# Separate semaphores for the loads of x and of the context, and x loaded one batch further ahead

## The chip, the cores and the metric

The kernel runs on one core of one Trainium2 chip. The metric is device time in microseconds (us), the median of three runs. The core has five engines that run their own instruction streams and meet only at semaphores: TensorE (PE in the profile, with its weight loads as PEld), VectorE (DVE), ScalarE (ACT), GpSimd (POOL) and SyncE (SP), which here does nothing but issue transfers (DMAs). An engine's queue, in which its waits and transfer issues stand, is written with a q, as SPq.

## The reference, cut to what matters

```
x = x + attention(layernorm(x), context, context, bias)   # 64 batches, 128 rows x 128; 16 heads of 64
x = x + moe_ffn(layernorm(x))                             # 8 experts of 128 -> 512 -> 128, 32 rows each
```

The 64 batches come as four groups of 16 to the expert layer's expert choice (the x of a batch is 128 rows by 128 columns, its context 120 rows by 128). In the attention, of each batch: q is made of the normalized x; k and v of the context; scores = q kT x 128^-0.5 + bias; softmax over the 120 columns; times v; and a projection back to 128 columns, added to x. The expert layer routes rows by a softmax over 8 logits and the top 32 rows per expert and batch. Everything is held to float32 accuracy, which the kernel reaches with pairs of float16 parts (hi and lo) and three products for one.

## The kernel before, in words

The program has two parts. The attention (function `attention`, lines 74 to 677) goes over the 64 batches; then come routing and the experts, which the change does not touch. The whole of x stays on the chip in `x_sb` (128 rows x 64 batches x 128), so the load of one batch's x has no buffer to wait for. The context of a batch goes to `ctx_f`, which has two buffers, taken in turn.

The attention is a software pipeline written out by hand. Each engine runs slots t = -1 to 68, and a slot has four steps g = 0 to 3, one for each group of four heads. Slots 5 to 62 or so are a loop whose body is two slots. What an engine does in a step is in fixed order, and belongs to several batches at once. In slot t:

- DVE begins step 0 with `bn_stats` of the x of batch t+1 (line 453). Before it stands a wait on `loaded_xc` (line 449). Then in every step: bias and row minimum of the scores (`neg`, line 461, four of them), the reciprocal of the softmax's sum (L498), the low part of v (L503), the attention's output (L518), and at the end of the step the low part of the probabilities of the step before (L545), which sets `p_lo_ready`.
- POOL raises the variance to the power -1/2 (`rstd`, L311), then waits on the same `loaded_xc` (line 314) and splits the context of batch t+1 into hi and lo (L318, L325). It also writes the high part of the probabilities (L288) and the low part of the output (L296).
- ACT does the exponentials (L432) and copies results out of PSUM.
- PE does in each step the scores (L593), v (L578 to L580 into `bk_b`), the projection of an older batch (L620), probabilities times v (L636), and q and k (L578 to L580 into `bk_a`). The projection and probabilities times v need transposed operands, `w_f`.
- SP issues, in slot t and step g, one transposing transfer `w_f<-parts` (L248): it turns the probabilities of batch t-1 and the outputs of an older batch. It waits for four semaphores, of which `p_lo_ready` is that of DVE's line 545. PE uses the result four steps later. Between the transposing transfers SP issues the ordinary loads: after the first (g = 0) the x and then the context of batch t+2 (`load_x`, lines 208 to 217), after the second (g = 1) a piece of the expert weights (`load_ffn`, L227).

Both loads of a batch count on one semaphore, `loaded_xc`, 32 for a batch, so DVE and POOL each wait for both of them. `load_x` itself waits at its head until both loads of all earlier batches have landed, and before the context until the buffer is free (`ctx_ready`). The function `alone` puts an empty instruction after a wait. Below, T0 to T3 are the four transposing transfers of a slot.

Of the kernel before, what the change touches and what calls it, by code (L numbers as in the profile page):

```python
# [73 lines left out]
def attention(nc, v):  # L74
    x, ctx_t, bias, wqkv_t, wp_t, gate_t, ffn_w = (v[n] for n in (
        "x", "ctx_t", "bias", "wqkv_t", "wp_t", "gate_t", "ffn_w"))
# [3 lines left out]
    x_sb, xg_hi, xg_lo, ffn_hi, ffn_lo, logits, ident, ident_h, iota, gate_sb = (v[n] for n in (  # L80
        "x_sb", "xg_hi", "xg_lo", "ffn_hi", "ffn_lo", "logits", "ident", "ident_h", "iota", "gate_sb"))

    with ExitStack() as ctx:
# [3 lines left out]
        def two(name, shape, dt):  # L87
            return [sb(f"{name}{i}", shape, dt) for i in range(2)]
# [4 lines left out]
        sem = v["sem"]  # L93
# [8 lines left out]
        ctx_f = two("ctx_f", [D, K], F32)  # L102
# [35 lines left out]
        xn_turned, x2_turned, gate_out = bk_m[:, 0:128].bitcast(F16), bk_m[:, 128:256], bk_m[:, 256:256 + E]  # L138

        loaded_wv, loaded_wq, loaded_wk = sem("loaded_wv"), sem("loaded_wq"), sem("loaded_wk")  # L140
        loaded_b, loaded_xc, loaded_ffn = sem("loaded_b"), sem("loaded_xc"), sem("loaded_ffn")

        weight_parts = ((loaded_wv, slice(2 * HD, 3 * HD)), (loaded_wq, slice(0, HD)), (loaded_wk, slice(HD, 2 * HD)))
        const_ready = sem("const_ready")
# [28 lines left out]
        def live(b):  # L173

            return not isinstance(b, int) or 0 <= b < B

        def upto(count):

            return min(count, B) if isinstance(count, int) else count

        def some(count):

            return not isinstance(count, int) or count > 0

        def alone(eng):

            eng.nop(nofuse=True)

        def slots(eng, slot, end=last, loop_end=loop_end, first=first):

            for t in range(first, FRONT):
                slot(t, t % 2)
            with eng.Fori(FRONT, loop_end - 1, 2) as t:
                slot(t, FRONT % 2)
                slot(t + 1, (FRONT + 1) % 2)
            for t in range(loop_end, end):
                slot(t, t % 2)

        def behind(t, g, k):

            return t - 1 + (g - k) // GROUPS, (g - k) % GROUPS
# [3 lines left out]
        @block.sync  # L205
        def _(sp):

            def load_x(b, par):

                if some(b):  # L210
                    sp.wait_ge(loaded_xc, 32 * b)
                    alone(sp)
                sp.dma_start(x_sb[:, b, :], x[:, b, :]).then_inc(loaded_xc, 16)
                if some(b - 1):
                    sp.wait_ge(ctx_ready, b - 1)
                    alone(sp)
                sp.dma_start(ctx_f[par][:, :], ctx_t[:, b, :]).then_inc(loaded_xc, 16)

            def load_ffn(b, par):

                if some(b):
                    sp.wait_ge(loaded_ffn, 16 * b)
                if some(b - 1):
                    sp.wait_ge(ffnw_ready, b - 1)
                alone(sp)
                src = ffn_w[:, bass.ds(b * WCH, WCH)] if not isinstance(b, int) else ffn_w[:, b * WCH:(b + 1) * WCH]
                sp.dma_start(wst[par][:, :], src).then_inc(loaded_ffn, 16)  # L227

            def turn(t, g):

                n = 4 * (t - 1) + g
                b5, g5 = behind(t, g, PV_LAG)
                blocks = slice(0 if live(t - 1) else 2 * GH, BLOCKS)
                if not live(t - 1) and not live(b5):
                    return
                if live(t - 1):
                    sp.wait_ge(p_lo_ready, n + 1)
                    alone(sp)
                    if some(n - GROUPS + 1):
                        sp.wait_ge(pv_written, n - GROUPS + 1)  # L240
                    alone(sp)
                if live(b5):
                    sp.wait_ge(o_lo_ready, 4 * b5 + g5 + 1)
                    alone(sp)
                    if some(4 * b5 + g5 - GROUPS + 1):
                        sp.wait_ge(proj_written, 4 * b5 + g5 - GROUPS + 1)
                    alone(sp)
                sp.dma_start_transpose(turned[g][:, blocks, :], parts[g][:, blocks, :].rearrange("p a b -> p (a b)")  # L248
                                       ).then_inc(moved[g], 16)

            def slot(t, par):
                for g in range(GROUPS):
                    turn(t, g)
                    if g == 0 and live(t + 2):
                        load_x(t + 2, par)
                    if g == 1 and live(t + 1):
                        load_ffn(t + 1, (par + 1) % 2)

            load_x(0, 0)
            slots(sp, slot, end=B + 3, loop_end=loop_end - 2)  # L260

        @block.gpsimd
        def _(pool):
# [26 lines left out]
            def lower_o(t, g):  # L290

                b5, g5 = behind(t, g, SPLIT_LAG)
                if live(b5):
                    n = 4 * b5 + g5
                    pool.wait_ge(o_hi_ready, n + 1)
                    pool.tensor_tensor(o_parts[g5][:, 1, :, :], o_sb[g5 % 2][:, :, :], o_parts[g5][:, 0, :, :],  # L296
                                       ALU.subtract).then_inc(o_lo_ready, 1)

            def slot(t, par):
                c = chain(t)  # L300
                i = (par + 1) % 2
                lower_o(t, 0)

                pool.wait_ge(vpe_ready, t + 2)
                alone(pool)
                if some(upto(t + 1)):
                    pool.wait_ge(xn_ready, upto(t + 1))
                if some(t - 4):
                    pool.wait_ge(xn2_ready, t - 4)
                alone(pool)  # L310
                pool.tensor_tensor(rstd[:, :], vpe[:, :], half[:, :], ALU.pow).then_inc(rstd_ready, 1)  # L311
                if live(t + 1):

                    pool.wait_ge(loaded_xc, (t + 2) * 32)
                    if some(4 * t):
                        pool.wait_ge(v_written, 4 * t)
                    alone(pool)
                    pool.tensor_copy(ctx_hi[i][:, :], ctx_f[i][:, :]).then_inc(pool_chain, 1)  # L318
                upper_parts(t, 0)
                lower_o(t, 1)  # L320
                if live(t + 1):

                    pool.wait_ge(pool_chain, c[0])
                    alone(pool)
                    pool.tensor_tensor(ctx_lo[i][:, :], ctx_f[i][:, :], ctx_hi[i][:, :],  # L325
                                       ALU.subtract).then_inc(ctx_ready, 1)

                    pool.wait_ge(xn_ready, t + 2)
                    if some(t + 1):
                        pool.wait_ge(xT_written, t + 1)  # L330
                    alone(pool)
                    pool.tensor_copy(xn_hi[:, :], xn[:, :]).then_inc(pool_chain, 1)
                    pool.wait_ge(pool_chain, c[1])
                    alone(pool)
                    pool.tensor_tensor(xn_lo[:, :], xn[:, :], xn_hi[:, :], ALU.subtract).then_inc(xn_parts_ready, 1)
                upper_parts(t, 1)
                lower_o(t, 2)
                upper_parts(t, 2)
                lower_o(t, 3)
                if live(t - 4):  # L340

                    pool.wait_ge(xg_hi_ready, t - 3)
                    alone(pool)
                    pool.tensor_tensor(xg_lo[:, t - 4, :], xn2[:, :], xg_hi[:, t - 4, :],
                                       ALU.subtract).then_inc(xg_ready, 1)
                upper_parts(t, 3)

            def chain(t):

                hi = 2 * (t + 1) if not isinstance(t, int) else 2 * min(t + 1, B)
                return [1 + hi + (k if live(t + 1) else 0) for k in (1, 2)]

            slots(pool, slot)

        @block.scalar
# [82 lines left out]
        def _(dve):  # L440
            dve.wait_ge(const_ready, 11)

            def step(t, par, g):
# [2 lines left out]
                tw, gw, pw = (t, g - 1, par) if g else (t - 1, GROUPS - 1, (par + 1) % 2)  # L446
                if g == 0 and live(t + 1):

                    dve.wait_ge(loaded_xc, (t + 2) * 32)
                    if some(t + 1):  # L450
                        dve.wait_ge(stats_ready, t + 1)
                    alone(dve)
                    nc.vector.bn_stats(stats[:, 0, :], x_sb[:, t + 1, :]).then_inc(x_stats_ready, 1)
# [98 lines left out]
            def slot(t, par):  # L552
                for g in range(GROUPS):
                    step(t, par, g)
# [734 lines left out]
```

## Time and profile before

| what | value |
|---|---|
| median of three runs | 1084.17 us (1082.05 to 1084.37) |
| the profiled execution | 1082.19 us |
| its span, first to last instruction | 1080.4 us |
| mean granted clock of TensorE | 0.975 of full speed |
| attention, steady stretch looked at | 100 to 640 us from the span's start, 49 slots |
| busy there, of 540 us | PE 527.1, DVE 523.2, ACT 483.5, POOL 385.3 |

A row of instructions gives the line, the engine, the operation, what it writes and reads, how often, the busy time and the mean duration, and then the idle time of the engine just before these instructions and what ended it. Records of one engine overlap where the next instruction begins before the last has drained, so sums of durations run above the busy time. A row of waits gives the waiting engine and line, what it waited for, the total, the number of times and the longest.

### The profile page before, as it was taken

What the parts mean: (1) busy time and instruction counts of PE and PEld (TensorE: products, weight loads), DVE (VectorE), ACT (ScalarE), POOL (GpSimd) and SP (SyncE); (2) the same over time, 40 slices, a digit from 0 to 9 for tenths busy, and PEclk for the clock granted to TensorE, in tenths of its full rate; (3) what the DMA queues carried; (4) which work ended last, traced back from release to release, by engine and by line L of the source; (5) the groups of instructions that cost most, each with busy time, mean ns of one, the idle gap of its engine ahead of it and who ended that gap; (6) DMA issues with size and microseconds to landing.
All of it is one profiled execution on the core that took longest, in us unless ns stands there. A gap on an engine that the chain in (4) does not pass through costs nothing. (4 is left out here: it accounts for less than half of the span.)

```text
span 1080.4 us, 47391 instructions
## 1 busy us (share of the span) xinstructions
PE 1001.7 (93%) x13640; PEld 810.5 (75%) x13640; DVE 895.2 (83%) x3981; ACT 839.0 (78%) x2536; POOL 724.7 (67%) x1086
## 2 busy tenths in 40 slices
PE   4999999999999999999999999983799999999995
PEld 3777888888888888888888888872466666666664
DVE  4999999999999999999999999995756565665553
ACT  5888898888988898888889899881576666666562
POOL 6677677777767676776767676772077667677673
PEclk9999999999999999999999999995599999999998
DMA  3998887888888887888888888892001121111112
GB/s 102 167 149 158 164 169 153 163 166 163 162 163 163 164 168 153 167 164 165 160 162 166 165 165 156 172 162 45 1 21 29 31 69 29 47 48 32 50 49 69
DMA packets 440585, 130.91 MB, mean 121 GB/s; under 512 B 417504, under 2 KB 433888, under 8 KB 440544
## 3 DMA queue, kind: packets, MB, share of 16 engines
q1 hardware_dynamic: 439680, 128.24, 61.0%
q10 hardware_dynamic: 864, 2.16, 0.5%
q8 instruction: 21, 0.34, 0.1%
q14 instruction: 20, 0.16, 0.0%
HBM read 16.58 MB, written 4.19 MB: 19 GB/s over the span
## 5 line engine op out<-in xcount | busy, mean ns | idle before, releaser
L432 ACT ACTIVATE probs<-neg,negmax 128x120 f32<-128x120 f32 x1024 | 320.4, 387 | 76.6 <-DVE negmax L461 76.1
L461 DVE CUSTOM_DVE_ANT_0 neg<-bk_s,bias_sb 128x120 f32<-128x120 f32 x1024 | 226.2, 275 | 3.3 <-PE bk_s L593 2.2
L1136 POOL TENSOR_TENSOR hid<-hid_f,hid 128x512 f16<-128x512 f32 x128 | 167.7, 1314 | 74.4 <-ACT hid L1090 73.4
L288 POOL CAST parts<-probs 128x480 f16<-128x480 f32 x256 | 151.9, 593 | 95.2 <-ACT probs L432 95.2
L296 POOL TENSOR_TENSOR parts<-o_sb,parts 128x256 f16<-128x256 f32 x256 | 172.0, 672 | 48.8 <-ACT parts L397 48.8
L593 PE MATMUL bk_s<-qk 64*128 64x120 f32 x2048 | 181.4, 294 | 8.7 <-DVE negmax L461 4.2
L545 DVE TENSOR_TENSOR parts<-probs,parts 128x480 f16<-128x480 f32 x256 | 171.3, 669 | 0.0
L593 PEld LDWEIGHTS bk_s<-qk 64*128 64x128 f32 x2048 | 136.7, 186 | 32.6 <-issue 13.6
L1190 DVE TENSOR_TENSOR hid_f<-bk_u,silu 128x512 f32<-128x512 f32 x128 | 88.4, 691 | 85.7 <-ACT silu L1083 35.0
L389 ACT COPY qk<-bk_a 128x496 f32<-128x496 f32 x256 | 146.5, 572 | 2.3 <-PE bk_a L580 2.3
L311 POOL TENSOR_TENSOR rstd<-vpe,half 128x2 f32<-128x2 f32 x69 | 77.2, 1118 | 68.2 <-DVE vpe L512 68.2
L636 PE MATMUL bk_o<-v_hi,w_f 120*128 120x65 f16 x1024 | 121.1, 196 | 1.1 <-DMA w_f<-parts 1.1
L638 PE MATMUL bk_o<-v_hi,w_f 120*128 120x65 f16 x1024 | 120.5, 193 | 0.0
L637 PE MATMUL bk_o<-v_lo,w_f 120*128 120x64 f16 x1024 | 120.0, 192 | 0.0
L578 PE MATMUL bk_a<-xT,w_hi 128*128 128x128 f16 x512 | 113.9, 222 | 5.0 <-ACT qk L389 2.2
L620 PE MATMUL bk_y<-wp_hi,w_f 128*128 128x128 f16 x512 | 100.7, 222 | 15.9 <-DMA w_f<-parts 14.7
L1083 ACT ACTIVATE silu<-bk_g 128x512 f32<-128x512 f32 x128 | 78.2, 611 | 44.3 <-PE bk_g L973 42.9
L580 PE MATMUL bk_a<-xT,w_hi 128*128 128x128 f16 x512 | 112.4, 220 | 0.0
L579 PE MATMUL bk_a<-xT,w_lo 128*128 128x128 f16 x512 | 112.3, 219 | 0.0
L1090 ACT CAST hid<-hid_f 128x512 f16<-128x512 f32 x128 | 80.7, 630 | 39.5 <-DVE hid_f L1190 39.2
L397 ACT CAST parts<-o_sb 128x256 f16<-128x256 f32 x256 | 105.9, 414 | 6.7 <-DVE o_sb L518 6.7
L579 PE MATMUL bk_a<-ctx_hi,w_lo 128*128 128x120 f16 x512 | 111.0, 217 | 0.0
(165 smaller groups left out, 3562.9 us busy)
## 6 DMA issues: line engine op xcount, KB each, us to landing
y_all<-y SPq DMA_DIRECT2D x128, 64.0 KB, 2.0
wst<-ffn_w SPq DMA_DIRECT2D x64, 96.0 KB, 2.6
w_f<-parts SPq DMA_TRANSPOSE x260, 3.7
x_sb<-x SPq DMA_DIRECT2D x64, 64.0 KB, 2.3
out<-x_sb SPq DMA_DIRECT2D x16, 256.0 KB, 2.0
ctx_f<-ctx_t SPq DMA_DIRECT2D x64, 60.0 KB, 2.0
w_f<-wqkv_t ACTq DMA_DIRECT2D x3, 512.0 KB, 5.4
wp_sb<-wp_t ACTq DMA_DIRECT2D x1, 512.0 KB, 5.9
```

What stands on the lines that cost most here:

```text
L288: pool.tensor_copy(p_parts[g][:, 0, :, 0:K], probs[g % 2][:, :, :]).then_inc(p_hi_ready, 1)
L296: pool.tensor_tensor(o_parts[g5][:, 1, :, :], o_sb[g5 % 2][:, :, :], o_parts[g5][:, 0, :, :], ALU.subtract).then_inc(o_lo_ready, 1)
L389: nc.scalar.copy(qk[pw][:, gw, :], bk_a[:, 0:QK]).then_inc(qk_ready, 1)
L432: e = nc.scalar.activation(probs[g % 2][:, i, :], neg[g % 2][:, i, :], ACT.Exp, bias=negmax[g % 2][:, i:i + 1], scale=-1.0)
L461: r = nc.vector.tensor_tensor_reduce(out=neg[g % 2][:, i, :], in0=bk_s[i % 2][:, (i // 2) * K:(i // 2 + 1) * K], in1=bias_sb[:, :], scale= ...
L545: nc.vector.tensor_tensor(p_parts[g1][:, 1, :, 0:K], probs[g1 % 2][:, :, :], p_parts[g1][:, 0, :, 0:K], ALU.subtract).then_inc(p_lo_ready, 1)
L579: nc.tensor.matmul(out, ll, rh, start=False, stop=False)
L593: m = nc.tensor.matmul(bk_s[h][:, j * K:(j + 1) * K], qk[p1][r, g, j * S:(j + 1) * S], qk[p1][r, g, GP * S + j * K:GP * S + (j + 1) * K], ...
L636: nc.tensor.matmul(bk_o[:, i * OW:(i + 1) * OW], ph, v_hi[p2][0:K, h, :], start=True, stop=False)
L637: nc.tensor.matmul(bk_o[:, i * OW:i * OW + DH], ph, v_lo[p2][0:K, h, :], start=False, stop=False)
L638: m = nc.tensor.matmul(bk_o[:, i * OW:(i + 1) * OW], pl, v_hi[p2][0:K, h, :], start=False, stop=True)
L1136: nc.gpsimd.tensor_tensor(hid[1][par][:, ic, :], hid_f[ic % 2][:, :], hid[0][par][:, ic, :], ALU.subtract).then_inc(hid_lo_ready, 1)
```

## The change

The semaphore `loaded_xc` becomes two, `loaded_x` and `loaded_ctx`, 16 a batch each. DVE waits on `loaded_x` alone, POOL on `loaded_ctx` alone. The function `load_x` is cut in two. `load_ctx` stays behind the first transposing transfer (g = 0) and loads the context of batch t+2 as before. `load_x` goes behind the fourth (g = 3) and loads the x of batch t+3, so that an x is issued three steps later in the slot but for one batch further on: it comes one step earlier than before with respect to the batch it serves. Each of the two waits until the earlier loads of its own kind have landed. Before the slots, SP issues x of batch 0, context of batch 0, and x of batch 1.

```diff
-            def load_x(b, par):
+            def load_x(b):
                 if some(b):
-                    sp.wait_ge(loaded_xc, 32 * b)
+                    sp.wait_ge(loaded_x, 16 * b)
                     alone(sp)
-                sp.dma_start(x_sb[:, b, :], x[:, b, :]).then_inc(loaded_xc, 16)
+                sp.dma_start(x_sb[:, b, :], x[:, b, :]).then_inc(loaded_x, 16)
+
+            def load_ctx(b, par):
+                if some(b):
+                    sp.wait_ge(loaded_ctx, 16 * b)
+                    alone(sp)
                 if some(b - 1):
                     sp.wait_ge(ctx_ready, b - 1)
                     alone(sp)
-                sp.dma_start(ctx_f[par][:, :], ctx_t[:, b, :]).then_inc(loaded_xc, 16)
+                sp.dma_start(ctx_f[par][:, :], ctx_t[:, b, :]).then_inc(loaded_ctx, 16)
...
                     if g == 0 and live(t + 2):
-                        load_x(t + 2, par)
+                        load_ctx(t + 2, par)
                     if g == 1 and live(t + 1):
                         load_ffn(t + 1, (par + 1) % 2)
-
-            load_x(0, 0)
+                    if g == 3 and live(t + 3):
+                        load_x(t + 3)
+
+            load_x(0)
+            load_ctx(0, 0)
+            load_x(1)
...
-                    pool.wait_ge(loaded_xc, (t + 2) * 32)
+                    pool.wait_ge(loaded_ctx, (t + 2) * 16)
...
-                    dve.wait_ge(loaded_xc, (t + 2) * 32)
+                    dve.wait_ge(loaded_x, (t + 2) * 16)
```

SP's program in the second slot of the loop's body, before: the last two transposing transfers of one slot (T2's end and T3 stand ahead of it), then T0 of the slot shown is the last `DMA_TRANSPOSE` before the loads, and T1 the one behind them.

```order
L237 ISA
L240 REGISTER_ALU [waits p_lo_ready]
L248 DMA_TRANSPOSE w_f<-parts 128x12x128 [waits pv_written,o_lo_ready,proj_written]
L211 ISA
L213 ISA [waits loaded_xc]
L213 DMA x_sb<-x 128x128
L217 ISA [waits ctx_ready]
L217 DMA ctx_f<-ctx_t 128x120
L237 REGISTER_ALU
L240 REGISTER_ALU [waits p_lo_ready]
L248 DMA_TRANSPOSE w_f<-parts 128x12x128 [waits pv_written,o_lo_ready,proj_written]
```

The same place now, from the load of x behind T3 of the slot before, over T0, to T1 (lines are 1 to 11 higher in the changed kernel).

```order
L212 ISA
L214 ISA [waits loaded_x]
L214 DMA x_sb<-x 128x128
L244 ISA
L247 REGISTER_ALU [waits p_lo_ready]
L255 DMA_TRANSPOSE w_f<-parts 128x12x128 [waits pv_written,o_lo_ready,proj_written]
L224 ISA [waits loaded_ctx,ctx_ready]
L224 DMA ctx_f<-ctx_t 128x120
L244 REGISTER_ALU
L247 REGISTER_ALU [waits p_lo_ready]
L255 DMA_TRANSPOSE w_f<-parts 128x12x128 [waits pv_written,o_lo_ready,proj_written]
```

The load of x has left the place between T0 and T1 and stands ahead of T0; the context is now directly behind T0, with one wait more.

SP's program from its start to the first transposing transfer, before.

```order
L213 DMA x_sb<-x 128x128
L217 DMA ctx_f<-ctx_t 128x120
L213 DMA x_sb<-x 128x128 [waits loaded_xc]
L217 DMA ctx_f<-ctx_t 128x120
L227 DMA wst<-ffn_w 128x192
L213 DMA x_sb<-x 128x128 [waits loaded_xc]
L217 DMA ctx_f<-ctx_t 128x120 [waits ctx_ready]
L227 DMA wst<-ffn_w 128x192 [waits loaded_ffn]
L248 DMA_TRANSPOSE w_f<-parts 128x12x128 [waits p_lo_ready]
```

And now.

```order
L214 DMA x_sb<-x 128x128
L224 DMA ctx_f<-ctx_t 128x120
L214 DMA x_sb<-x 128x128 [waits loaded_x]
L224 DMA ctx_f<-ctx_t 128x120 [waits loaded_ctx]
L234 DMA wst<-ffn_w 128x192
L214 DMA x_sb<-x 128x128 [waits loaded_x]
L224 DMA ctx_f<-ctx_t 128x120 [waits loaded_ctx,ctx_ready]
L234 DMA wst<-ffn_w 128x192 [waits loaded_ffn]
L214 DMA x_sb<-x 128x128 [waits loaded_x]
L255 DMA_TRANSPOSE w_f<-parts 128x12x128 [waits p_lo_ready]
```

Four loads of x instead of three stand ahead of the first transposing transfer, and each load waits for the earlier ones of its kind alone.

## Rows read from the trace of the kernel before

**Rows 1.** Stage 100 to 640: engines' busy time as headed, granted clock, DMA share, GB/s.

```profile
core 0: us, PE busy (x) PEld busy (x) DVE busy (x) ACT busy (x) POOL busy (x), PEclk, DMA share, GB/s
100.00:640.00 540.00, 527.12 (x8270) 463.90 (x8267) 523.18 (x2791) 483.49 (x1615) 385.25 (x685) 1.00 0.85 163
```

**Rows 2.** Groups of DVE's instructions, 100 to 640 us: the first of a slot.

```profile
L453 DVE BATCH_NORM_STATS2 stats<-x_sb 128x6 f32 x49 | 14.4, 295 | 16.2 <-DMA ctx_f<-ctx_t 15.2 <-issue 0.7
```

**Rows 3.** Who waited for whom, 100 to 640 us: total us, times, longest.

```profile
ACT probs L432 <- DVE negmax L461: 56.5, 98, 1.0
POOL rstd L311 <- DVE vpe L512: 43.0, 49, 1.3
...
PEld bk_y L620 <- DMA w_f<-parts: 16.5, 48, 0.7
DVE stats L453 <- DMA ctx_f<-ctx_t: 15.2, 40, 0.6
PEld bk_s L593 <- issue: 8.7, 36, 0.4
PEld bk_a L578 <- ACT qk L389: 6.1, 34, 0.2
```

**Rows 4.** Who waited for the loads of `ctx_f`, whole span: us, times.

```profile
  DVE stats L453: 19.4, 47
```

**Rows 5.** DVE in order of time, end of one slot and start of the next.

```profile
304.73 0.74 DVE L545 TENSOR_TENSOR parts<-probs,parts 128x480 f16<-128x480 f32 x1
...
309.71 0.64 DVE L545 TENSOR_TENSOR parts<-probs,parts 128x480 f16<-128x480 f32 x1
310.60 0.29 DVE L453 BATCH_NORM_STATS2 stats<-x_sb 128x6 f32 x1 [0.25 <-DMA ctx_f<-ctx_t]
310.92 0.28 DVE L461 CUSTOM_DVE_ANT_0 neg<-bk_s,bias_sb 128x120 f32<-128x120 f32 x1
```

**Rows 6.** SP's queue in order of time: T0 to T3 and the next T0.

```profile
305.77 1.43 SPq L248 DMA_TRANSPOSE w_f<-parts  x1
307.54 0.58 SPq L213 DMA_DIRECT2D x_sb<-x  x1
308.36 0.33 SPq L217 DMA_DIRECT2D ctx_f<-ctx_t  x1
309.09 1.41 SPq L248 DMA_TRANSPOSE w_f<-parts  x1
310.82 0.63 SPq L227 DMA_DIRECT2D wst<-ffn_w  x1
311.84 1.44 SPq L248 DMA_TRANSPOSE w_f<-parts  x1
...
313.68 1.48 SPq L248 DMA_TRANSPOSE w_f<-parts  x1
...
316.97 1.42 SPq L248 DMA_TRANSPOSE w_f<-parts  x1
```

**Rows 7.** SP's own waits, 100 to 640 us.

```profile
SPq L187 <- DVE parts L545: 47.6, 61, 1.2
```

**Rows 8.** Transfers: KB of one, median us from issue to landing.

```profile
w_f<-parts SPq DMA_TRANSPOSE x260, 3.7
x_sb<-x SPq DMA_DIRECT2D x64, 64.0 KB, 2.3
...
ctx_f<-ctx_t SPq DMA_DIRECT2D x64, 60.0 KB, 2.0
```

**Rows 9.** PE in order of time: scores of step 3 and of the next step 0.

```profile
306.81 0.71 PE L593 MATMUL bk_s<-qk 64*128 64x120 f32 x8
...
309.68 0.71 PE L593 MATMUL bk_s<-qk 64*128 64x120 f32 x8 [0.15 <-issue]
...
310.69 0.22 PE L620 MATMUL bk_y<-wp_hi,w_f 128*128 128x128 f16 x1
```

**Rows 10.** DVE and POOL in order of time: first scores of step 3; split of the context.

```profile
307.77 0.27 DVE L461 CUSTOM_DVE_ANT_0 neg<-bk_s,bias_sb 128x120 f32<-128x120 f32 x1
...
302.91 0.28 POOL L318 CAST ctx_hi<-ctx_f 128x120 f16<-128x120 f32 x1
```

More of the change, by code:

```diff
@@ L140, in attention @@
         loaded_wv, loaded_wq, loaded_wk = sem("loaded_wv"), sem("loaded_wq"), sem("loaded_wk")
-        loaded_b, loaded_xc, loaded_ffn = sem("loaded_b"), sem("loaded_xc"), sem("loaded_ffn")
+        loaded_b, loaded_ffn = sem("loaded_b"), sem("loaded_ffn")
+        loaded_x, loaded_ctx = sem("loaded_x"), sem("loaded_ctx")
         weight_parts = ((loaded_wv, slice(2 * HD, 3 * HD)), (loaded_wq, slice(0, HD)), (loaded_wk, slice(HD, 2 * HD)))
```

## The prediction

> **What bounds the kernel now.** I first read the stages. From 100 to 640 us, PE is busy 527.1 us of 540 and DVE 523.2, at full clock [rows 1]; a slot takes 540 / 49 = 11.02 us (49 is the count of the first instruction of a slot) [rows 2]. Two engines at 97% leave the question which one waits for which, and a busy PE hides stalls, since the ends of its matmuls are modelled. So I next read who waited for whom. In this stretch DVE has one wait, ever: `bn_stats`, the first instruction of a slot, for the load of the context, 15.2 us in 40 of 49 slots [rows 3]. Its idle time there is 16.2 us [rows 2], and the stage leaves 540 - 523.2 = 16.8: DVE's stream is full but for this stall. The others have room: ACT waits 56.5 us for DVE, POOL 43.0 for DVE, PE 16.5 + 8.7 + 6.1 = 31.3 at its weight loads [rows 3]. DVE is the bound, with 0.33 us of stall in a slot.
>
> The reader should see in order of time what the stall is. DVE's step ends at 310.35, and `bn_stats` starts at 310.60 after 0.25 idle, released by the context [rows 5]. The x that it reads was issued at 307.54, the context at 308.36 [rows 6]; at medians of 2.3 and 2.0 us to landing [rows 8], x is there at 309.84 and the context at 310.36, when DVE is ready. DVE waits for a load that it does not read, since both count on one semaphore.
>
> **Part 1: DVE's wait for the context goes.** `bn_stats` now waits for x alone, and on the scale of rows 6 the x issued behind T3, at about 315.5, is for the `bn_stats` one slot after that at 310.60, so at about 321.3 (310.60 + 11.02 - 0.33): 5.8 us ahead, against 2.3 us to landing. The x is never late. In the steady stretch this frees 15.2 us; the 0.7 and the rest of the 16.2 that no transfer ends I leave standing. Outside it, 19.4 - 15.2 = 4.2 us [rows 4] lie in the filling and draining of the pipeline, where other waits are near; bounds 0 and 4.2, I take half, 2.1. Term: -17.3, at most 16.2 + 4.2 = 20.4.
>
> **What is late next on DVE's side.** Scores: PE's scores of step 0 end at 309.68 + 0.71 = 310.39, DVE takes them at 310.92, 0.53 later [rows 5, 9]. Less 0.33 this is 0.20. At step 3 they end at 307.52 and are taken at 307.77 [rows 9, 10], 0.25 later, and there DVE does not wait. So it just fits in this slot. Over a slot PE needs 11.02 less its own waits of 31.3 / 49 = 0.64, that is 10.38; DVE needs 11.02 - 0.33 = 10.69. PE can follow, by 0.31. If all its waits for transposed operands stayed (16.5 / 49 = 0.34), it would need 10.72 and the gain would be 0.30 in a slot for 0.33.
>
> **Part 2: the context moves up behind T0; POOL waits for it alone.** POOL splits it at 302.91, some 2.3 us into a slot [rows 10], and DVE waited for the same load before the slot began, so it has been there for over 2 us. It is issued about 0.8 us earlier now (308.36 against 307.54). Cost nothing; were the cover gone, POOL's 43.0 / 49 = 0.88 us of waiting a slot would come first.
>
> **Part 3: SP's queue.** SP is nearly full: it waits 47.6 us of 540 [rows 7], 0.97 a slot, so its issues take 10.05 of 11.02. Added: one more wait, bounded by 0 and by the whole gap between the end of x's issue and the context's, 308.36 - 308.12 = 0.24; I take 0.12, for the gap holds a wait of the same kind and other instructions. The context's issue, now right behind a transposing one, may take what x takes there (0.58) and not 0.33: 0 to 0.25, I take 0.25, since the weights' load behind T1 takes 0.63 too. That makes 10.42, at most 10.54: under DVE's 10.69. x's own issue fills a gap: from T3's end at 313.68 + 1.48 = 315.16 to the next T0 at 316.97 lie 1.81 us, where a transposing issue that waits for nothing needs about 0.40 (T2's end to T3) [rows 6]. x takes 0.34 + 0.58 = 0.92 with the gap ahead of it, the shorter slot takes 0.33: 0.16 us is left. T0 is held by DVE (its operand ends at 305.47 [rows 5], T0 starts at 305.77), so it does not get later. T1 and T2 come earlier behind T0 by the 0.82 from x's issue to the context's, less 0.25 and 0.12: 0.45. PE needs them 0.33 earlier. So they are no later for PE than now, and its 16.5 us of waits shrink rather than grow. Cost 0 by this, and 0.15 a slot if x's issue is as slow as its neighbours allow (rival one).
>
> Here the page "DMA: Bandwidth & Descriptors" of the Trainium skill (section Issuing engines are not separate DMA queues) says that the issue time on the sequencer is usually small beside the transfer. By that rule SP would never bind and rival one would have no chance. The trace disagrees: a transposing issue holds SP 1.43 us of 3.7 to landing [rows 6, 8], and four with three loads fill 91% of its time. I go by the trace.
>
> **Part 4: the start.** Four loads of x instead of three stand ahead of the first transposing transfer, each waiting for the one before: at most one more landing, 2.3 us, on a queue that waits for DVE then. I take 0, bounds -1 and +1.
>
> **Sum.** Against the profiled execution, 1082.19 us (span 1080.4, 1.8 around it): -17.3 and 0 give 1064.9. The median of the runs stands 2.0 above that execution, one run of three beside it; I add 1 and predict 1066.
>
> **Rivals.**
>
> One: SP or the transposed operands bind next, and about half is kept. For it: only 0.16 us is left ahead of T0, only 0.20 ahead of the scores of step 0. If x's issue and T0's waits come out 0.3 longer, T0 is 0.3 - 0.16, about 0.15, late in every slot and the slot becomes 10.69 + 0.15, so 0.18 a slot is gained: 49 x 0.18 = 9, with nothing at the ends: 1082.2 - 9 + 1 = 1074 (1070 to 1079). Against it: SP's work is 10.42 by the sum.
>
> Two: nothing changes, the stall passes to the scores (L593) or to another wait of DVE that the profile shows at zero because `bn_stats` took it first. For it: PE is 98% busy. Against it: PE waits 0.64 a slot, much of it for DVE itself. 1082 to 1085. That the change does not do what it says belongs here: x would have to be what ended the stall, and at 309.84 it was not.
>
> Three, slower: x now stands right ahead of T0, and T0's data wait for x's. T0 lands at 305.77 + 3.7 = 309.47, and PE needs it at 310.69 [rows 9]: 1.22 of room, 0.89 in the shorter slot. Beyond that delay PE starts late in every slot; from 0.89 + 0.33 = 1.22 on it costs more than is gained. If T0 waited for the whole landing of x, 2.3 less the 0.56 that x's issue ends before it, it would be 1.74 late: +0.52 a slot, 49 x 0.52 = 25, 1108. Against it: T1 stands right behind both loads today, and the median transposing transfer still lands in 3.7.
>
> The same page of the Trainium skill (section Queues, rings and completion order) says that a DMA engine takes descriptors of a queue in ring order. That speaks against the change; by it T0 waits while x's 64 KB move, at the stage's 163 GB/s [rows 1] an estimate of 0.4 us, which is under 0.89. It puts rival three's chance low.
>
> **How the numbers follow.** Forecast 0.65, rival one 0.23, two 0.07, three 0.05. The forecast alone would give 1061 to 1069: the whole 20.4 below, 13 above. The range that holds 8 in 10 takes in rival one's centre: 1060 to 1076. A measurement of this kernel tells 0.2% (2.2 us) from no change. Faster 0.88 (forecast and rival one), same 0.07, slower 0.05.
>
> **What would show it.** In the changed profile DVE's `bn_stats` has no wait for a transfer, and DVE's idle time from 100 to 640 us falls under 3 us; the slot is 10.7 us. The load of x stands between T3 and T0, T1 about 0.45 us earlier behind T0. PE's waits for `w_f` fall under 16.5 us. I am wrong if DVE's idle time comes back at `neg` (L461 before) behind PE, or if SP's waits for DVE fall to nearly nothing while PE waits longer for `w_f`.

## The result

The changed kernel takes 1057.4 us (median of 4 runs, 1056.93 to 1060.19); the kernel before 1084.16 (4 runs). The ratio is 0.9763, 95% interval 0.9742 to 0.9784, so 2.4% faster. A second time, beside the experiments, it took 1056.72 us (5 runs; the kernel before 1084.51 there), ratio 0.9753 (0.9739 to 0.9767). The forecast was 1066 with a range of 1060 to 1076: the direction was right, the time lies below the range. The profiled execution of the changed kernel is the slowest of its four, 1060.19 us with a span of 1058.4; that of the second time took 1055.92 with 1054.1.

From 100 to 640 us the stages show more work in the same time (50.8 slots for 48.9), columns as in [rows 1]:

```profile
100.00:640.00 540.00, 532.02 (x8590) 478.31 (x8588) 539.05 (x2900) 503.06 (x1678) 404.79 (x712) 1.00 0.88 169
```

DVE is busy 539.05 of 540 us, for 523.18 in [rows 1]. Its first instruction of a slot has lost its idle time, 16.2 us in [rows 2] (line 453 is now 464):

```profile
L464 DVE BATCH_NORM_STATS2 stats<-x_sb 128x6 f32 x51 | 14.4, 283 | 0.0
```

The waits of the same stretch, for [rows 3], and then SP's own, for [rows 7]:

```profile
POOL parts L299 <- ACT probs L443: 72.2, 102, 0.8
ACT probs L443 <- DVE negmax L472: 36.5, 101, 0.5
...
POOL rstd L322 <- DVE vpe L523: 23.1, 51, 0.7
PEld bk_y L631 <- DMA w_f<-parts: 15.3, 33, 0.8
PE bk_y L631 <- DMA w_f<-parts: 7.5, 25, 0.5
DVE rsum L509 <- PE bk_o L649: 0.4, 2, 0.2
```

```profile
SPq L188 <- DVE parts L556: 0.5, 3, 0.2
```

The row of DVE waiting for the context is gone; nothing of its size has taken its place on DVE. ACT and POOL wait less for DVE, which comes round sooner. SP waited 47.6 us for DVE before and waits 0.5 now: its queue is nearly without a pause.

In order of time, end of a slot on DVE, for [rows 5]:

```profile
290.45 0.63 DVE L556 TENSOR_TENSOR parts<-probs,parts 128x480 f16<-128x480 f32 x1
291.00 0.28 DVE L464 BATCH_NORM_STATS2 stats<-x_sb 128x6 f32 x1
291.21 0.26 DVE L472 CUSTOM_DVE_ANT_0 neg<-bk_s,bias_sb 128x120 f32<-128x120 f32 x1
```

The last operation of the slot (line 556, 545 before) starts at 290.45 and lasts to 291.08, and `bn_stats` starts at 291.00, before that end. In [rows 5] the same two starts lie 0.89 apart, here 0.55.

SP's queue, for [rows 6]: T0, context, T1, weights, T2 and T3 in one row, x, the next T0.

```profile
287.04 1.45 SPq L255 DMA_TRANSPOSE w_f<-parts  x1
288.95 0.46 SPq L224 DMA_DIRECT2D ctx_f<-ctx_t  x1
289.93 1.43 SPq L255 DMA_TRANSPOSE w_f<-parts  x1
291.69 0.61 SPq L234 DMA_DIRECT2D wst<-ffn_w  x1
292.80 3.31 SPq L255 DMA_TRANSPOSE w_f<-parts  x2
296.46 0.55 SPq L214 DMA_DIRECT2D x_sb<-x  x1
297.43 1.43 SPq L255 DMA_TRANSPOSE w_f<-parts  x1
```

T1 follows T0 after 2.89 us, 3.32 in [rows 6]. On average over the stage it is 2.82 us, 3.42 before. From one T0 to the next it is 10.39 us here and 11.20 there, but these two are unlike: the 11.20 holds the end of the loop's body, the 10.39 does not, and the next T0, behind the loop's end, comes after 10.76.

**Where the time went, slot by slot.** I measured from start to start on DVE, over the 49 slots of the stretch before and 50 after. A slot fell from 11.040 to 10.625 us, by 0.415. From the start of its last operation to the start of `bn_stats` it was 0.965 us and is 0.558: 0.407, nearly all of it. From `bn_stats` to the first `neg` 0.273 became 0.211, and the rest of the slot grew by 0.054, in steps 2 and 3, where DVE now and then is held by PE. The last `bn_stats` starts 23.4 us earlier in the profiled executions (697.1 and 673.7 us), 25.6 earlier in that of the second time (671.5). What follows the last `bn_stats` takes the same in all three, 383 to 385 us.

### The profile page after: what moved, and what is told of

Its sections match the earlier page's. It is cut to its first block and busy times, and to the rows that moved or that the text cites. A ratio compares the mean times of both kernels' runs of the same rounds, so it can differ in the third digit from the quotient of the medians.

```text
span 1058.4 us, 47454 instructions
## 1 busy us (share of the span) xinstructions
PE 984.5 (93%) x13640; PEld 808.5 (76%) x13640; DVE 889.0 (84%) x3981; ACT 840.1 (79%) x2536; POOL 727.7 (69%) x1086
## 5 line engine op out<-in xcount | busy, mean ns | idle before, releaser
L299 POOL CAST parts<-probs 128x480 f16<-128x480 f32 x256 | 155.4, 607 | 96.3 <-ACT probs L443 96.3
L591 PE MATMUL bk_a<-ctx_lo,w_hi 128*128 128x120 f16 x512 | 111.1, 217 | 0.0
L589 PE MATMUL bk_a<-ctx_hi,w_hi 128*128 128x120 f16 x512 | 111.1, 217 | 0.0
```

Of the source, the lines that this page charges most:

```text
L299: pool.tensor_copy(p_parts[g][:, 0, :, 0:K], probs[g % 2][:, :, :]).then_inc(p_hi_ready, 1)
L589: nc.tensor.matmul(out, lh, rh, start=True, stop=False)
L591: return nc.tensor.matmul(out, lh, rl, start=False, stop=True)
```

## The experiments

The theory that I had after reading the two traces (A): the gain is DVE's stall alone, and its price was larger than the idle time in the profile (the time in which the engine's records show nothing). Rivals: the excess comes from transposing transfers issued earlier (B), or only the new place of x matters (C); and, on what binds now, SP's full queue (S) against DVE alone. "The changed kernel" is after. Line numbers in experiments shift by a few.

**Semaphores parted, x in its old place.**

```diff
                     if g == 0 and live(t + 2):
+                        load_x(t + 2)
                         load_ctx(t + 2, par)
...
-                    if g == 3 and live(t + 3):
-                        load_x(t + 3)
...
-            load_x(1)
```

> Only the semaphores are parted: x and the context are both still issued behind the first transposing transfer, in the old order. Theory A (the whole gain is DVE's wait for the context, and a stall costs more than the idle time that the profile shows: 0.959 us from the start of DVE's last operation of a slot to its bn_stats before the change, 0.558 after it, though the idle time was 0.33): the wait is gone here too, since x lands half a us before DVE wants it; that interval falls to about 0.56 and the time to 1057 to 1063, the upper part if the later transposing transfers cost something. Rival B (what exceeds the 0.33 us comes from transposing transfers that are issued earlier since x stands elsewhere): the gain stays at 0.33 us a slot or less, 1064 to 1070. Rival C (the place of x is what matters): 1075 to 1084.

Measured: 1069.62 us, ratio 0.9857 (0.9838 to 0.9876). DVE no longer waits for a load (its stretch to `bn_stats` is 0.573 us), but the slot is 10.80:

```profile
PEld bk_y L629 <- DMA w_f<-parts: 25.0, 52, 0.7
...
PE bk_y L629 <- DMA w_f<-parts: 12.2, 48, 0.5
DVE rsum L507 <- PE bk_o L647: 7.4, 23, 0.5
```

So 14.9 of the 27 us come by the semaphores alone. The rest is not lost at `bn_stats`: with both loads between T0 and T1, the transposed operands reach PE late in steps 1 and 2 of the shorter slot (25.0 us of waits at the weight loads, for 16.5 in [rows 3]), and DVE waits for PE's product. The number is inside the expectation of B, yet its mechanism is not what I named there: the transposing transfers give no gain of their own, they are what binds next once DVE is free. My A had 1063 as its upper end and was wrong by 6.6 us.

**x moved, one semaphore kept.** Shown against the changed kernel, the waits alone; both loads count on `loaded_xc`.

```diff
-                    sp.wait_ge(loaded_x, 16 * b)
+                    sp.wait_ge(loaded_xc, 32 * b)
...
-                    sp.wait_ge(loaded_ctx, 16 * b)
+                    sp.wait_ge(loaded_xc, 32 * b + 16)
...
-                    pool.wait_ge(loaded_ctx, (t + 2) * 16)
+                    pool.wait_ge(loaded_xc, (t + 2) * 32)
...
-                    dve.wait_ge(loaded_x, (t + 2) * 16)
+                    dve.wait_ge(loaded_xc, (t + 2) * 32)
```

> Only the place of x is changed: x goes behind the fourth transposing transfer, a batch further ahead, but both loads count on the one semaphore as before and DVE still waits for the context too. Theory A: the context, now directly behind the first transposing transfer, lands about 0.5 us earlier, before DVE wants it; no stall, 1057 to 1060. Rival C': if the parting of the semaphores is what does it, DVE still waits at bn_stats and the time stays at 1075 to 1084.

Measured: 1063.31 us, ratio 0.9812 (0.9798 to 0.9826): 21.2 us by the place alone, 3 above what A expected. The profile shows hardly any idle time left at `bn_stats`:

```profile
L464 DVE BATCH_NORM_STATS2 stats<-x_sb 128x6 f32 x51 | 14.8, 290 | 2.7 <-DMA ctx_f<-ctx_t 1.2 <-issue 0.4
```

2.7 us over 51 slots are 0.05 a slot, but the stretch to `bn_stats` is 0.649 us, 0.091 over the changed kernel's, and the slot 10.70. In order of time, a slot without any idle time marked and one with it:

```profile
303.28 0.64 DVE L556 TENSOR_TENSOR parts<-probs,parts 128x480 f16<-128x480 f32 x1
303.99 0.30 DVE L464 BATCH_NORM_STATS2 stats<-x_sb 128x6 f32 x1
...
324.75 0.64 DVE L556 TENSOR_TENSOR parts<-probs,parts 128x480 f16<-128x480 f32 x1
325.64 0.29 DVE L464 BATCH_NORM_STATS2 stats<-x_sb 128x6 f32 x1 [0.26 <-DMA ctx_f<-ctx_t]
```

The first lost 0.15 us against 0.56 and carries no mark: 0.07 of it is idle time (303.92 to 303.99) that this view does not print, the rest is overlap with the last operation. The second lost 0.33 and is marked with 0.26. The two parts of the change overlap: 14.9 + 21.2 = 36.1, and together they gave 27.8 beside the same runs of the kernel before.

**Both waits, with the changed kernel's order of loads.**

```diff
                     dve.wait_ge(loaded_x, (t + 2) * 16)
+                    dve.wait_ge(loaded_ctx, (t + 2) * 16)
```

> The changed kernel with its own order of loads, in which DVE's bn_stats waits for the context again beside x. In the kernel with only x moved, DVE had almost no idle time at bn_stats (1.6 us in 540), yet the stretch from its last operation's start to bn_stats was 0.65 us for 0.558, and the slot 10.70 for 10.62. Theory A (a wait that ends while the last operation still drains costs the overlap of the two, some 0.08 us, though no idle time shows): the same here, slot 10.70, 1061 to 1064. Rival (SP's own waits, which on one semaphore hold the context until x has landed, are what cost there): no cost here, slot 10.62, 1056 to 1058.

Measured: 1067.14 us, ratio 0.9846 (0.9831 to 0.9861), slot 10.78: theory A in kind, though 3 us above its range; the rival's range is missed by 9. The stretch to `bn_stats` is 0.728 us, 0.17 over 0.558, where the profile marks 6.1 us of idle time over 50 slots, 0.12. The other 0.05 a slot carry no mark:

```profile
L465 DVE BATCH_NORM_STATS2 stats<-x_sb 128x6 f32 x50 | 14.6, 292 | 6.1 <-DMA ctx_f<-ctx_t 3.1 <-issue 2.0
```

So at the new place the parting of the semaphores is still worth 10 us: the context, right behind T0, takes 2.4 us to land (median) for 2.0 behind x, and arrives about when DVE wants to start. Why one semaphore for both (1063.3) is 4 us better than two with both waits stays open.

**The stall made long.** The kernel before, its context issued behind the second transposing transfer.

```diff
                 sp.dma_start(x_sb[:, b, :], x[:, b, :]).then_inc(loaded_xc, 16)
+
+            def load_ctx(b, par):
+
                 if some(b - 1):
...
+                    if g == 1 and live(t + 2):
+                        load_ctx(t + 2, par)
```

> The kernel before (one semaphore, both waits) with the context issued behind the second transposing transfer, not the first, to make DVE's stall at bn_stats long, some 2.4 us. Theory A (a stall costs its idle time and a constant 0.08 to 0.15 us for the overlap lost): slot = 10.63 + idle + 0.08 to 0.15. Rival (a stall costs in proportion, 0.41 for 0.33, or 1.25 times the idle time): slot = 10.63 + 1.25 x idle, so 0.5 us a slot more than A at 2.4 us. The time at 2.4 us of idle: 1210 to 1225 by A, 1240 to 1260 by the rival.

Measured: 1249.96 us (2 runs), ratio 1.153, inside the range that I gave the rival. But the stall is longer than I had reckoned for either (2.77 us for 2.4), and the granted clock is lower, 0.938 over the span for 0.975, so the time itself tells little between the two. The stretch does:

```profile
L459 DVE BATCH_NORM_STATS2 stats<-x_sb 128x6 f32 x40 | 11.8, 295 | 110.6 <-DMA ctx_f<-ctx_t 110.6
```

```profile
305.65 0.64 DVE L551 TENSOR_TENSOR parts<-probs,parts 128x480 f16<-128x480 f32 x1
309.20 0.29 DVE L459 BATCH_NORM_STATS2 stats<-x_sb 128x6 f32 x1 [2.92 <-DMA ctx_f<-ctx_t]
```

Idle 110.6 / 40 = 2.77 us a slot, stretch 3.401 on average; 3.401 - 0.558 - 2.766 = 0.077. In the kernel before: 0.965 - 0.558 - 0.330 = 0.077. The price of a stall is its idle time and 0.077 us, at a stall eight times as long: the proportional rival (0.558 + 1.25 x 2.77 = 4.02) falls. That the two 0.077 agree is less than it seems: once a stall outlasts the last operation's record, the sum gives that record's length less 0.558, and the two runs show only that the length stays (3.401 - 2.766 and 0.965 - 0.330, both 0.635). The slot is 13.68, 0.2 over A's 13.5, against 14.1 by the rival; over half of the excess is idle time elsewhere in the slot, where DVE waits 3.5 us for PE's products and 1.5 for its scores in 40 slots.

**x in pairs of batches.**

```diff
-                    if g == 3 and live(t + 3):
+                    if g == 3 and par == 1 and live(t + 3):
...
-                sp.dma_start(x_sb[:, b, :], x[:, b, :]).then_inc(loaded_x, 16)
+                pair = slice(b, b + 2) if isinstance(b, int) else bass.ds(b, 2)
+                sp.dma_start(x_sb[:, pair, :], x[:, pair, :]).then_inc(loaded_x, 16)
```

> The changed kernel, with x loaded for two batches at a time, so that every other slot has no load of x in SP's queue. In the changed kernel SP waits for DVE 0.5 us in 540 in all, and PE's waits for the transposed operands hold DVE for about 0.07 us a slot. If SP's queue is what holds the slot there now (theory S): 0.07 x 59 = 4 us less than the changed kernel, 1053, SP has waits again and PE's waits for w_f fall. If DVE alone holds it (rival): the same as the changed kernel within 1 us.

Measured: 1057.27 us (1055.44 to 1059.96), ratio 0.9762 (0.9745 to 0.9779): no gain. SP has its waits back and PE its operands:

```profile
SPq L188 <- DVE parts L556: 33.4, 45, 1.2
```

```profile
PEld bk_y L631 <- DMA w_f<-parts: 6.7, 27, 0.4
...
PE bk_y L631 <- DMA w_f<-parts: 0.3, 2, 0.2
```

But the slot is 10.637 us, for 10.625 and 10.618 in the two profiles of the changed kernel. DVE has no wait in the profile there, so its own stream is that long, though not all of it is work: its slots alternate between 10.80 us at the head of the loop's body and 10.47, and in the first two short pauses follow, one before the first `neg` and one before the reciprocal (L509), 0.14 and 0.13 us more than in the second. In the first profile of the changed kernel the two slots take 10.57 and 10.68: there the second is lengthened where DVE is held by PE, and the head costs less.

**Four empty instructions more on SP** behind the first transposing transfer.

```diff
+                    if g == 0:
+                        for _ in range(4):
+                            alone(sp)
                     if g == 0 and live(t + 2):
```

> The changed kernel with four empty instructions more in SP's queue in every slot, behind the first transposing transfer, some 0.2 us. Loading x in pairs took 0.46 us a slot off SP and gained nothing, so DVE is at its floor. If SP, which shows no wait there, has no room either, the slot grows by the most of 0.2: 1064 to 1069, with more waits of PE for w_f and of DVE for PE. If SP has room that its few waits hide: 1056 to 1059.

Measured: 1058.26 us. It tells nothing: the program has no more instructions on SP than the changed kernel's. The two traces hold 3115 of SP's records each, of the same kinds, and from T0's end to the context's issue SP takes 0.375 us in both. The four empty instructions wait for nothing and never became part of the program, so this was the changed kernel once more, and what an empty instruction costs stays unknown.

**One load more on SP.**

```diff
                         load_x(t + 3)
+                        if some(t + 1):
+                            sp.wait_ge(loaded_more, 16 * (t + 1))
+                            alone(sp)
+                        sp.dma_start(more[:, :], x[:, 0, :]).then_inc(loaded_more, 16)
```

> The changed kernel with one load more in every slot, behind that of x, of 64 KB into a buffer that nobody reads: some 0.57 us of issue and 0.4 around it on SP, 0.95 a slot. (The four empty instructions of the run before had left no trace in SP's queue, so it told nothing.) If SP has no room beside DVE in the changed kernel, as its missing waits say (theory S), the slot grows by all of it, 10.62 to 11.5, and the time by 0.95 x 59 = 56 to 1105 to 1115. If SP has room r that its waits do not show, the slot grows by 0.95 - r: with r = 0.4, by 0.55, 1085 to 1095; with r over 0.9 nothing, 1057.

Measured: 1086.99 us, ratio 1.003 (1.0016 to 1.0044), slot 11.13. By the number this is r = 0.45 of room, and that reading is wrong: the load does not cost 0.95 on SP. Behind x it takes 0.39 and 0.10 of gap, 0.49 in all:

```profile
306.42 0.56 SPq L215 DMA_DIRECT2D x_sb<-x  x1
307.07 0.39 SPq L271 DMA_DIRECT2D more<-x  x1
307.88 1.42 SPq L256 DMA_TRANSPOSE w_f<-parts  x1
```

The slot grew by 0.50, and SP has no wait left in the stretch. Slower transfers are no rival: the transposing ones land after 3.66 to 3.88 us on average, 3.66 to 3.80 in the changed kernel, and the DMA engines are busy for 0.86 of the time, 0.88 there. So SP has no room in the changed kernel: S is right that it binds, and the pairs show that DVE's stream binds at the same length. The two limits coincide within 0.02 us a slot; the runs show no reason why they should.

**A loop body of four slots, with x in pairs.**

```diff
-            with eng.Fori(FRONT, loop_end - 1, 2) as t:
+            with eng.Fori(FRONT, loop_end - 3, 4) as t:
```

> x in pairs, and the loop's body of four slots for two. With x in pairs DVE waits for nobody, and its slots alternate between 10.80 and 10.47 us, the longer one at the head of the loop's body. If the head costs these 0.33 us, a body of four slots has it half as often: 0.08 us a slot, 4 to 5 us less than in pairs, 1051 to 1054. If the alternation has another cause, the time stays at 1056 to 1059.

Measured: 1130.39 us, ratio 1.0445 (1.0426 to 1.0465). Two of four slots take 10.47 us, as the shorter ones do in pairs, but the other two 13.3 and 13.5, with waits that no other engine ends:

```profile
DVE stats L464 <- issue: 32.6, 12, 3.6
PEld bk_s L604 <- issue: 32.6, 30, 3.2
...
DVE mv L488 <- issue: 20.3, 11, 2.0
```

The page's queue of instructions carries 92 packets there for 20 in the changed kernel:

```profile
q14 instruction: 92, 0.75, 0.2%
```

The instructions of the longer body are fetched anew, it seems; I read that from the two counts and did not test it apart. What the 0.33 us at the loop's head are stays open: this run was to tell and cannot. No kernel that I ran beats the changed one.

## Why the prediction was right, and where it was wrong

**Right: the bound and the mechanism.** DVE's stream was full but for the wait, DVE waited for a load that it does not read, x is never late, POOL does not wait for the context, and the stall did not pass to the scores. DVE's idle time is 0.95 us (under 3 was forecast) and the slot 10.62 us (10.7). The rival that nothing changes is refuted by `bn_stats`' idle time of 0.0, the slower one by T0's landing (median 3.7 us still).

**Wrong: the size of the stall, term -17.3, "at most 20.4".** Two things in it failed. First, I took the idle time (0.33 a slot) for the price, which was 0.407. Where nothing waits, `bn_stats` starts 0.08 us before the record of the operation ahead of it ends; behind a wait that overlap is lost, and the profile books it as busy. The rows showed it: `bn_stats` started 0.89 us after the last operation in [rows 5], where 0.64 less the overlap is 0.56, so the stall there cost 0.33 with 0.25 marked. With 47 stalls [rows 4] that is 3.6 us; it puts the whole stall at 19.4 + 1.1 (the share that no transfer ended, over the whole span) + 3.6 = 24.1 us, over my upper bound, against 23.4 and 25.6 measured up to the last `bn_stats`. Second, I kept too much back: the rest of the idle time that no transfer ends I left standing, and outside the steady stretch I halved 4.2. The steady stretch gave 0.415 x 49 = 20.3 us for my 15.2, and the filling and draining the remaining 3 to 5 for my 2.1, though new waits of DVE for PE appear in the filling.

The Trainium skill, page "Perfetto Trace Analysis" (Summary: the profiler window per engine type), says that a DVE record runs from execution to the acknowledged write. A next record that begins before the last one ends, as in these traces, fits that; the 0.077 us are this case's.

**Partly right: SP's queue.** I reckoned 10.42 us, at most 10.54, and 0.15 of room under DVE. One load more went into the slot whole, 0.50 for 0.49: SP has no room at 10.62. What I missed stands in [rows 6]: I took 0.40 us, T2's end to T3, for the gap ahead of T0, but in every second slot SP's branch back to the loop's head lies there. In the changed kernel x's end to T0 is 0.42 us without the branch (296.46 + 0.55 to 297.43, above) and 1.05 on average with it:

```profile
306.58 0.55 SPq L214 DMA_DIRECT2D x_sb<-x  x1
308.19 1.42 SPq L255 DMA_TRANSPOSE w_f<-parts  x1
```

That is 0.63 us where I had counted 0.16 of room, 0.31 a slot on average. T1 came 0.43 us earlier behind T0 in the rows shown (3.32 to 2.89; 0.45 predicted; 0.60 on average). PE's waits for `w_f` at the weight loads fell from 16.5 to 15.3, as forecast, but those at the matmuls rose to 7.5 from this row of the kernel before:

```profile
PE bk_y L620 <- DMA w_f<-parts: 4.7, 20, 0.4
```

So of the second sign of being wrong, SP's waits gone and PE waiting longer for `w_f`, the first half came whole and the other in part. Rival one was right on what comes next and wrong on the price, since DVE's floor is met at the same length. That the move of x matters for PE was in the sum only as "no later than now": parted semaphores alone show its worth, 12 to 13 us (1069.6 against 1057.4 and 1056.7). And rival two's "much of it for DVE itself" is not what [rows 3] book: of PE's 31.3 us, 16.5 are for transfers, 8.7 for issue and 6.1 for ACT.

**The last 1 us.** I added 1 for the median, and the changed kernel's median lies 2.8 us below its profiled execution. The stage from 0 to 100 us, in the changed kernel's profile and in that of the second time:

```profile
0.00:100.00 100.00, 78.65 (x1154) 68.45 (x1155) 79.37 (x398) 76.91 (x232) 63.50 (x117) 0.98 0.80 143
```

```profile
0.00:100.00 100.00, 79.40 (x1191) 69.11 (x1191) 81.47 (x413) 78.73 (x238) 65.98 (x119) 1.00 0.83 147
```

In the filling the first was granted 0.98 of the clock, the second and the kernel before all of it; DVE did 15 instructions fewer there. By the spans the gain is 22.0 us with the first profile, 26.3 with the second; the medians say 26.8 and 27.8. Why that execution differs was not tested.

## What to carry to other kernels

Price a stall from start to start, against the same pair of instructions where nothing waits: the idle time that a profile marks leaves out what the next instruction would have overlapped, and a wait that ends in that overlap costs time with no mark at all. Give each consumer a semaphore of what it reads, but look first at who comes next: here the waiting engine, the transfer queue and the operands for PE lay within about 0.4 us of each other in a slot of 11, and the two halves of the change alone gave 15 and 21 of 27 us. Before filling a gap in a queue, look for the loop's end in it. And here, once the queue had lost its last wait, one more transfer in it cost its full issue time.

## What the hardware showed that I had not expected

- An ordinary transfer's issue on SP takes 0.57 to 0.67 us on average right behind a transposing one, and 0.33 to 0.39 right behind another ordinary one; the context's landing goes from 2.0 to 2.4 us when it moves up behind the transposing transfer.
- Where the loop's end lies between x's issue and T0, SP needs 1.05 us between them, and 0.42 elsewhere.
- A loop body of four slots for two made two slots of four 2.9 us longer, at 92 packets of the instruction queue for 20; the cause was not tested.
